# A transformer decoder on one core: how the operand area of its attention scores is laid out, cleared and filled

## The reference, cut to what matters

```python
x = x + _L0_attn_ref(_layernorm(x), ...)       # linear attention with random features
x = x + _L0_xattn_ref(_layernorm(x), ctx, ctx, mask, ...)   # softmax, 16 heads of 8
x = x + _L0_ffn_ref(_layernorm(x), ...)        # 4 binary trees of 256 leaves, gathered leaf by leaf
x = x + _L1_attn_ref(_layernorm(x), ...)       # causal softmax, 16 heads of 8
x = x + _L1_xattn_ref(_layernorm(x), ctx, ...) # softmax, 16 heads of 8
x = x + _L1_ffn_ref(_layernorm(x), ...)        # product keys, top 16 of 1024 experts per head
```

```python
scores = jnp.einsum('bhqd,bhkd->bhqk', qh, kh) * scale      # d = 8
```

## Time and profile before

| | |
|---|---|
| median of 3 runs | 845.75 us (842.77 to 845.91) |
| the profiled execution | 847.52 us, its span 845.8 us |
| mean granted clock of TensorE | 0.877 of full |
| PE / DVE / ACT / POOL busy | 683.9 / 593.8 / 435.9 / 300.8 us |
| first run, second run | about 124 to 212 us, 479 to 642 us |
| DMA issues of `parts` | 144 of 64.0 KB, all from SP |
| DMA issues of the pads | 6 of 1232.0 KB, all from SP |

### The profile page before, as it was taken

How to read it: one execution, slowest core, us unless ns; L and a number is a source line. 1 busy time by engine, 2 the same in 40 slices (tenths; PEclk the granted TensorE clock), 3 DMA queues, 4 the chain that set the end, 5 groups by cost and what they waited for, 6 DMA issues and landing times. The chain is left out here.

```text
span 845.8 us, 14575 instructions
## 1 busy us (share of the span) xinstructions
PE 683.9 (81%) x4864; PEld 515.3 (61%) x4864; DVE 593.8 (70%) x2447; ACT 435.9 (52%) x1046; POOL 300.8 (36%) x309
## 2 busy tenths in 40 slices
PE   3876887798737989888778777999987878888888
PEld 1435533454316776777667655765544667788888
DVE  5584537573459797997579645788754788899984
ACT  1122012466108877788856424556664665555562
POOL 3010841200043323233113102212100578888883
PEclk9887556999558899999979768999998989999999
DMA  8700041320078969699745633333300000000000
GB/s 256 157 1 2 1 57 26 45 36 2 0 309 312 393 251 384 252 370 399 264 163 213 163 88 45 55 51 50 43 2 1 0 2 4 4 4 5 4 5 7
DMA packets 42675, 93.64 MB, mean 111 GB/s; under 512 B 4050, under 2 KB 30194, under 8 KB 34408
## 3 DMA queue, kind: packets, MB, share of 16 engines
q0 software_dynamic: 9216, 69.47, 21.5%
q1 hardware_dynamic: 33384, 23.23, 14.1%
HBM read 74.42 MB, written 0.52 MB: 89 GB/s over the span
## 5 line engine op out<-in xcount | busy, mean ns | idle before, releaser
L799 ACT ACTIVATE arena<-arena,hact 128x128 f32<-128x128 f32 x512 | 155.0, 388 | 1.0
L595 POOL TENSOR_TENSOR arena<-arena 128x1024 f32<-128x1024 f32 x64 | 121.1, 1913 | 22.0 <-DVE arena L1259 16.5
L692 ACT ACTIVATE arena<-psum 128x512 f32<-128x512 f32 (+1 forms) x192 | 101.1, 561 | 53.5 <-PE psum L1417 52.6
L1120 DVE CUSTOM_DVE_ANT_0 arena<-arena,fx 128x128 f32<-128x128 f32 x384 | 105.9, 343 | 0.3
L1753 PE MATMUL psum<-arena 128*128 128x128 f32 x688 | 89.2, 289 | 18.2 <-DVE arena L1259 11.3
L850 ACT ACTIVATE psum<-arena,tneg 128x1024 f32<-128x1024 f32 x64 | 71.5, 1118 | 61.8 <-DVE arena L1259 29.1
L930 DVE TENSOR_REDUCE rowmax<-psum 128x2 f32<-128x512 f32 x128 | 81.5, 686 | 29.1 <-PE psum L1399 27.0
L1753 PEld LDWEIGHTS psum<-arena 128*128 128x128 f32 x688 | 84.7, 203 | 21.0 <-DVE arena L1259 13.2
L1633 PE MATMUL psum<-identf,arena 128*128 128x128 f32 x544 | 75.8, 295 | 23.4 <-ACT arena L799 23.0
L1399 PE MATMUL psum<-arena 128*128 128x256 bf16 (+1 forms) x384 | 77.0, 294 | 18.5 <-DVE rowmax L930 10.1
L1633 PE MATMUL psum<-arena,identf 128*128 128x128 f32 x544 | 79.4, 300 | 15.4 <-ACT arena L799 14.1
(11 more groups left out here) (229 smaller groups left out, 1181.1 us busy)
## 6 DMA issues: line engine op xcount, KB each, us to landing
arena<-parts SPq DMA_DIRECT2D x144, 64.0 KB
arena<-zeros SPq DMA_DIRECT2D x6, 1232.0 KB
w_sb<-attn_w SPq DMA_DIRECT2D x1, 768.0 KB, 8.3
x<-x_in SPq DMA_DIRECT2D x1, 512.0 KB, 4.4
fx<-ctx_in SPq DMA_DIRECT2D x1, 512.0 KB, 5.5
picked<-mask_in SPq DMA_DIRECT2D x1, 512.0 KB, 6.8
wq_sb<-peer_wq SPq DMA_DIRECT2D x1, 512.0 KB, 7.4
down_sb<-table_down SPq DMA_DIRECT2D x1, 512.0 KB, 8.4
```

Source lines behind the costliest of these rows:

```text
L595: nc.gpsimd.tensor_tensor(grid[k % 3].rearrange("p (i j) -> p i j", i=PK), sim[:, t, h, :].unsqueeze(2).to_broadcast([P, PK, PK]), sim[:, ...
L692: nc.scalar.activation(probs[k % (2 * HG)][:, 0:w], bank(2 + k % 2, 0, w), ACT.Exp, scale=float(D) ** -0.5).then_inc(probs_ready, 1)
L799: a = nc.scalar.activation(w, w, ACT.Copy, scale=hact[i % 2][:, l:l + 1])
L1120: i = nc.vector.tensor_tensor_reduce(w, w, src, 1.0, r[:, LW * E + l:LW * E + l + 1], ALU.mult, ALU.add, hid[g % 4][:, l:l + 1])
```

## The change

The six terms of an area are interleaved: term r's feature d goes to partition r + 16 d instead of 8 r + d, the maxima and ones to partitions 6, 22 and 38. The zeros of the whole area (all 128 partitions) come from a memset on GpSimd, `clear(i)`, and no longer from a DMA of SP: areas 1 and 2 early, area 0 behind `power(6)`, and for the second run all three behind `power(10)`. The ones are placed just ahead of each item's `place`. From the third item of a run on, SP issues only the six transfers of part 0; the other six are issued from ScalarE's queue behind the exponentials of heads 5 to 8 of item n-2.

```diff
-KS = len(TERMS) * D
-KM = KS + 3
+NT = len(TERMS)
+ROWS = P // D
...
-        stk_pad = [aw[KM:P, i * STK:(i + 1) * STK].rearrange("p (j n) -> p j n", n=4 * S) for i in range(3)]
+        max_rows = [i[NT:NT + 2 * ROWS + 1:ROWS] for i in stk]
...
-            def place(n):
+            def place(n, parts_here=3):
 
                 if n - 3 >= B:
                     sp.wait_ge(cols_ps, (n - 3 - B + 1) * H)
-                sp.dma_start(stk[n % 3][KS:KM, :, 0, :],
-                             zeros[0:KM - KS, 0:S].unsqueeze(1).to_broadcast([KM - KS, H, S])).then_inc(stk_ready[n % 3], 16)
-                for part, ready in enumerate((part0_ready, part1_ready, parts_ready)):
+                if n - run_of(n)[0] < 3:
+                    sp.wait_ge(clear_ready[n % 3], 1 if n < 2 * B else 2)
+                sp.dma_start(max_rows[n % 3][:, :, 0, :],
+                             zeros[0:3, 0:S].unsqueeze(1).to_broadcast([3, H, S])).then_inc(stk_ready[n % 3], 16)
+                for part, ready in enumerate((part0_ready, part1_ready, parts_ready)[0:parts_here]):
                     sp.wait_ge(ready, n - B + 1)
                     for r, term in enumerate(TERMS):
                         for w in range(2):
                             if term[w] == part:
-                                sp.dma_start(stk[n % 3][r * D:(r + 1) * D, :, w, :],
+                                sp.dma_start(stk[n % 3][r:P:ROWS, :, w, :],
                                              parts[n % 2][:, part, w, :]).then_inc(stk_ready[n % 3], 16)
...
+            def fixed(n):
+
+                sp.wait_ge(clear_ready[n % 3], 1 if n < 2 * B else 2)
+                sp.dma_start(max_rows[n % 3][:, :, 1, :],
+                             ones[:, :].unsqueeze(1).to_broadcast([3, H, S])).then_inc(pad_ready[n % 3], 16)
...
-                else:
-                    sp.wait_ge(leaf_done, len(ORDER) - 2)
-                    pad(first % 3)
+                fixed(first)
                 place(first)
...
+                fixed(first + 1)
                 place(first + 1)
                 place_max(first)
+                fixed(first + 2)
                 for n in range(first, last + 1):
                     if n + 2 <= last:
-                        place(n + 2)
+                        place(n + 2, 1)
...
+            def clear(i):
+
+                nc.gpsimd.memset(arena[:, i * (STK // 2):(i + 1) * (STK // 2)], 0.0).then_inc(clear_ready[i], 1)
+
+            clear(1)
+            clear(2)
             pool.wait_ge(kmax_ready, 1)
...
                 power(NEXT[-1] + 1)
+                pool.wait_ge(leaf_done, len(ORDER) - 2)
+                clear(NEXT[0] % 3)
+                pool.wait_ge(fh_ready, len(ORDER))
+                clear(NEXT[1] % 3)
+                clear((NEXT[1] + 1) % 3)
...
             power(B + 2)
+            pool.wait_ge(bias_ready, 2)
+            clear(0)
             run(*RUNS[0])
...
+            def place_rest(n, part, w):
+
+                if n - 3 >= B:
+                    act.wait_ge(cols_ps, (n - 3 - B + 1) * H)
+                act.wait_ge(part1_ready if part == 1 else parts_ready, n - B + 1)
+                for r, term in enumerate(TERMS):
+                    if term[w] == part:
+                        nc.scalar.dma_start(stk[n % 3][r:P:ROWS, :, w, :],
+                                            parts[n % 2][:, part, w, :]).then_inc(stk_ready[n % 3], 16)
...
+                        if n + 2 <= last and h in (5, 6):
+                            place_rest(n + 2, 1, h - 5)
+                        if n + 2 <= last and h in (7, 8):
+                            place_rest(n + 2, 2, h - 7)
```

16 lines of the change are left out of this document (3 added, 13 removed).

## The result

The changed kernel takes 850.36 us (median of 20 runs, 844.84 to 855.31), the kernel before, on the same chip, 845.91 (20 runs, 839.47 to 848.45). The ratio is 1.0046, with an interval of 1.0029 to 1.0064: 4 us slower. The forecast was 845 in 840 to 858. The time lies in the range, but "same" was the likeliest case, and the kernel is slower by a little less than the 0.5% that was set for it: single executions of the two kernels overlap, but the interval of the ratio lies wholly above 1. The range held only by the room that it left for a rival; the forecast's own 841 to 850 is just missed. The profiled execution took 847.38 us (span 845.6).

What follows compares the result with a forecast made beforehand. It took TensorE's standstills for the operand area `stk`, whose transfers land late, as the place to gain. Terms -3.1 - 5.6 - 5.9 - 0.8 + 10.2 + 4.4 = -0.8 gave 845 us, range 840 to 858.

Steps and rivals of the forecast that it cites:

- same: The case that the time differs from the kernel before by no more than about 0.5%; chance 0.46.
- the forecast's own 841 to 850: Range without the rivals: ScalarE's issues at 0.1 to 1.0 us a stage, the memset at 3.5 to 4.2 us.
- Step 1: Transfers into rows 16 apart: about 0.5 us each, below the 0.66 of an issue, so no backlog forms.
- Rival A: Transfers into rows 16 apart stay at 0.89 us each; 862 us in all; chance 0.17.
- Step 2: First score product of n=4: operands land before TensorE asks, so the whole wait of 3.06 us goes, -3.1.
- Step 3: Starts of n=6 and n=10, with ScalarE issuing half the transfers: waits go, -5.6 and -5.9, later stages -0.8.
- Step 4: Start of the second run: memset behind `power(10)`, then ones, zeros and transfers delay TensorE, +10.2 us.
- Step 5: The clears at the start and behind `power(6)` fit in GpSimd's idle time and cost nothing.
- Step 6: ScalarE's six issues in each of 8 stages delay exponentials: 0.55 us a stage, +4.4 us.
- Rival C: ScalarE's issues are hidden and cost nothing: 840.5 us, just faster; chance 0.15.
- rival B: ScalarE's issues lie fully on the path: 1.5 us a stage, +12.0 instead of +4.4, 852.5 us; chance 0.13.

Runs made afterwards that it cites:

- run 7: The kernel before, with its old rows and clearing transfers, but six of the twelve transfers issued from ScalarE's queue after heads 5 to 8: 847.4 us, ratio 1.0009.
- run 1: The changed kernel, but SP issues all twelve transfers of a stage and ScalarE none: 841.02 us, ratio 0.9936 against the kernel before.
- run 3: The changed kernel with the memset of area 2 moved ahead of `power(10)`, the other two still behind it: 844.35 us, ratio 0.9974 against the kernel before.
- run 2: The changed kernel with the memset of area 0 moved ahead of `power(6)`: 847.07 us, ratio 1.0002 against the kernel before.
- run 6: The kernel before, with only two GpSimd memsets of 128x3072 added behind `power(6)`, into an unused part of the arena: 849.27 us, ratio 1.0038.
- Runs 11 and 12: The changed kernel: in 11 one small input loads from ScalarE's queue at the start, 850.85 us; in 12 ScalarE issues the first part, SP the rest, 849.41 us.
- run 8: The changed kernel with ScalarE's four groups of issues behind heads 8 to 11 instead of 5 to 8: 847.49 us, ratio 1.0024 against the kernel before.

## Why the forecast was wrong, step by step

*Step 1, rows 16 apart: right.* Transfers below 0.66 us were forecast and the issue is the bound; how far below it they lie these windows can't show. Rival A (they stay at 0.89) is refuted by the windows.

*Step 2, n=4: right, a little too much.* 2.4 us came back (3.06 to 0.67) of the 3.1.

*Step 3, n=6 and n=10: the gain is there, the means were not needed.* From head 14 to the next head 0 it is 3.5 us at n=4 (161.0 to 164.5), against 9.1: 5.6 less, as said. At n=8 it is 3.0 (521.1 to 524.1) against 9.4. Yet part of that is TensorE coming later, as in run 7: heads 0 to 14 of n=4 take 19.0 us in the changed kernel and took 14.9. Whole stages of run 1, which has the new rows and none of ScalarE's issues, show the gain unmixed: n=4 19.6 instead of 24.0, n=8 16.6 instead of 23.5, the other stages 1.5 less together. That is 12.7 us, where the forecast had 5.6 + 5.9 + 0.8 = 12.3. But the step put ScalarE's half of the transfers into the account as necessary. Run 1 has 0.25 and 0.47 us of wait without it. The layout alone does it, and run 7 shows the other half alone gaining nothing in sum.

*Step 4, the start of the second run: right.* Gap 12.12 (12 to 13 said), memset behind `power(10)` at 470.22, 3.5 us each. From the end of the last leaf to the first exponential it is 33.9 us, against 25.1: +8.8 instead of +10.2. The gap grew by 10.1 and not 10.7, the 0.89 of n=9 went as said, and the sixteen heads took 12.0 us against 12.3, where 0.4 was added. Run 3 takes 6 us of it away again.

*Step 5, clears at the start: this is the step that failed.* It said of clear(0): "POOL idles 6.74 us before 145.60 because the split waits for ScalarE: nothing", and named GpSimd's own queue as the only cover. GpSimd's queue had room indeed. What was not looked at is who else needs what a memset holds: it stands right behind `power(6)`, and `power(6)` is just what releases VectorE's scalings, so the two begin within 0.1 us of each other. +3.0 us in the trace, 3.7 by run 2, and shown by putting it into the old kernel in run 6. The forecast had 0. For clear(1) and clear(2) its "nothing" came true, but by luck: they held VectorE for 5.1 us at 60, and the three clears of step 4 held it for 9.9 at 470, which the forecast did not see either; both times nobody waited for it.

*Step 6, ScalarE's issues: right mechanism, wrong size; the other term that failed.* +4.4 said. Eight stages cost 8.0 us by the stages of run 1, 9.3 by its time. The six issues cost 0.7 to 0.9 a stage, not 0.55, seven times. And the eighth, n=4, costs 2.8, which the step read from a late stage as well. What the rows give of the difference: 0.36 of wait for the split, 0.6 since the first issue of that stage takes 1.2 us in place of 0.61, and about 1 us of lower clock behind TensorE's waits. Runs 11 and 12 take away one suspect each and change the stage by 0.3 us or less; run 8 puts the issues two or three heads later and gets 2.5 back, with the clock. Whether these three add up as they stand is not shown. Rival C (hidden) is refuted, and rival B (1.5 us a stage) was too much: it is 1.0 on average, between the forecast and B. Why that one issue is long stays open: it is so in all seven profiled kernels in which ScalarE issues (the changed one and runs 2, 3, 7, 8, 11 and 12: 1.17 to 1.44 us), whatever the rows or the part; all later issues take 0.61 to 0.85.

The sum with the measured sizes: -2.4 (n=4) - 12.7 (stages, step 3) + 8.8 + 3.0 + 8.0 = +4.7, and the runs say +3.9 (2.5 to 5.4). The table has +5.8 for the same stretches, of which 1.0 is the last item of run 1, which takes 12.8 or 13.8 us whatever the kernel. Of the 5.5 us that the forecast lacked (it had -0.8) 3.0 are the memset's and 3.6 ScalarE's; the second start was 1.4 cheaper than said, and the gains came within 0.3 of the forecast. It could call "same" likeliest only since it summed gains and losses of 15 us each, where a few us on one side decide.

## What to carry to other kernels

An instruction that goes into an engine's idle time is free only if nothing it locks is wanted by another engine: look at what starts right beside it, above all where both are released by the same instruction. Issues in a compute engine's queue cost something in every pass (here six of 0.61 us cost 0.7 to 0.9), and more where that engine's reader has just begun to run short; before pricing it, ask whether the cheaper layout already made the second queue unnecessary. When a transfer touches few rows, spread both of its ends: source and target each set a rate of their own.

## What the runs showed of the hardware

- A GpSimd memset of 128x4096 f32 (3.51 us) held two VectorE scalings, which take 0.60 us, for 3.56; two back to back held two such scalings for 7.02 and three for 10.47; two with a semaphore wait between held them for one (2.71). An instruction on 128x2 took 1.89 instead of 0.17. VectorE's leaf products kept their 0.34. Sixteen row maxima out of PSUM took 11.05 with a memset beside the first of them and 11.04 without.
- Transfers of 64 KB into 8 neighbouring rows moved 74 GB/s; into rows 16 apart they kept pace with the issue, at 101 to 105. Transfers that read 8 neighbouring rows and wrote rows 16 apart moved 51, and with both ends 16 apart 114 to 122. The Trainium skill, page "SBUF — State Buffer", section "Door 1: The DMA port swizzle", gives 27.2 GB/s a port and by its map 2 ports to rows 0 to 7 and 4 to rows 16 apart: an estimate of 54 and 109. Reading 8 neighbours (51) agrees, both ends spread come out a little above, and writing into 8 neighbours (74) was faster than it allows.
- When transfers take longer than their issue, the issue comes to last as long as a transfer: 2.51 to 2.56 us each from the fourth on (21.16 us for ten, where ten issues cost 6.6).
- Behind standstills of 4.38 and 4.44 us TensorE's granted clock read 0.60 and 0.50 in the next 4 us; behind 1.59 and 2.10 us at the same places (run 7) it read 1.00.
